# Layer norm of a four-layer graph network: five parts, squares with the mean as bias, subtraction and scaling in one operation

## The reference

```python
def _layernorm(x, axis=-1, eps=1e-05):
    m = jnp.mean(x, axis=axis, keepdims=True)
    v = jnp.var(x, axis=axis, keepdims=True)
    return (x - m) / jnp.sqrt(v + eps)

h = jnp.maximum(_layernorm(x, axis=-1), 0.0)
x = x + _L0_gnn_ref(h, edge_weight, edge_index)          # weighted means over edges, both directions
h = jnp.maximum(_layernorm(x, axis=-1), 0.0)
x = x + _L1_gnn_ref(h, ...)                              # graph convolution, top-2 mixture of 64 experts, batch norm
h = jnp.maximum(_layernorm(x, axis=-1), 0.0)
x = x + _L2_gnn_ref(h, src, dst, L2_gnn_betas)           # four layers of attention by cosine
h = jnp.maximum(_layernorm(x, axis=-1), 0.0)
x = x + _L3_gnn_ref(h, edge_index, ...)                  # three layers of graph attention, four heads
return x
```

## Time and profile before

| what | value |
|---|---|
| median of three runs | 10631.17 us |
| lowest, highest | 10622.68, 10632.24 us |
| the profiled execution's own time | 10520.32 us |
| its span | 10518.6 us |
| mean granted TensorE clock | 0.817 of full speed |
| busy: PE, PEld, DVE, ACT, POOL | 6449.8, 5108.4, 5163.6, 3005.7, 5412.2 us |

### The profile page before, as it was taken

One profiled execution on the slowest core, in us unless ns is written; L12 is line 12 of the kernel. 1 busy time (PEld: TensorE's weight loads), 2 busy tenths in 40 slices (PEclk: granted clock), 3 DMA queues, 4 the chain that ended last, 5 costly groups with the idle time before them and its releaser, 6 DMA issues. The chain is left out here.

```text
span 10518.6 us, 150096 instructions
## 1 busy us (share of the span) xinstructions
PE 6449.8 (61%) x33804; PEld 5108.4 (49%) x33805; DVE 5163.6 (49%) x13884; ACT 3005.7 (29%) x7335; POOL 5412.2 (51%) x5498
## 2 busy tenths in 40 slices
PE   0004434434464872886778688588668868876886
PEld 0003334423342762665666566466546545654554
DVE  7002223341113224555555555555657757775777
ACT  0000000000001221333333333333345545554554
POOL 2766666646641112564555455455436645654563
PEclk9996666666665996998898799899878888888888
DMA  3201113343330981334334333433323333333333
GB/s 135 71 8 41 40 46 85 87 67 93 91 57 22 334 294 49 84 84 74 80 82 81 73 84 82 73 81 82 61 71 82 80 69 78 80 76 67 80 79 66
DMA packets 614773, 886.37 MB, mean 84 GB/s; under 512 B 285685, under 2 KB 423161, under 8 KB 613408
## 3 DMA queue, kind: packets, MB, share of 16 engines
q0 software_dynamic: 241344, 609.84, 26.3%
q1 hardware_dynamic: 373344, 275.70, 8.7%
HBM read 757.50 MB, written 134.33 MB: 85 GB/s over the span
## 5 line engine op out<-in xcount | busy, mean ns | idle before, releaser
L1557 POOL DMA_INDIRECT hs<-tab_agnn,rec x1952 | 1886.2, 966 | 1676.0 <-issue 530.5
L1998 POOL DMA_INDIRECT hs<-tab_gat,rec x1464 | 1516.0, 1036 | 1083.9 <-issue 499.5
L1621 DVE CUSTOM_DVE_ANT_0 prod<-psG,hs 128x256 f32<-128x256 f32 x1952 | 836.3, 481 | 1007.3 <-remote 523.1
L1680 PE MATMUL psG<-HN,ohT 128*128 x3904 | 1097.5, 426 | 109.2 <-DVE lg L1621 74.0
L2030 DVE TENSOR_REDUCE mt<-psL 128x2 f32<-128x1024 f32 x732 | 873.3, 1219 | 477.8 <-remote 208.9
L1697 PE MATMUL psV<-hs,pr 128*128 128x258 f32 x3904 | 1006.6, 404 | 3.3 <-DVE acc L1604 3.3
L1680 PEld LDWEIGHTS psG<-HN,ohT 128*128 128x128 f32 x3904 | 772.8, 210 | 257.4 <-DVE lg L1621 96.6
L2163 PE MATMUL psV<-msg,oh 128*128 128x260 f32 x2928 | 824.5, 431 | 7.2 <-issue 6.8
L1697 PEld LDWEIGHTS psV<-hs,pr 128*128 128x128 f32 x3904 | 759.2, 205 | 104.4 <-DVE acc L1604 4.9
L661 PE MATMUL psT<-ident,oh 128*128 128x128 f32 x488 | 125.1, 406 | 1095.3 <-issue 837.2
L1636 ACT ACTIVATE prT<-cand,mn 128x512 f32<-128x512 f32 x488 | 352.4, 722 | 1519.0 <-DVE mn L1582 1143.3
(11 more groups left out here) (324 smaller groups left out, 12837.2 us busy)
## 6 DMA issues: line engine op xcount, KB each, us to landing
w<-in_L_gnn_w SPq DMA_DIRECT2D x224, 512.0 KB, 5.8
fwd_d<-acc SPq DMA_DIRECT2D x10, 3172.0 KB
fw<-fwd_d SPq DMA_DIRECT2D x122, 260.0 KB
hs<-tab_agnn,rec POOLq DMA_INDIRECT x1952
hs<-tab_gat,rec POOLq DMA_INDIRECT x1464
rec<-rec_d SPq DMA_DIRECT2D x1220, 8.0 KB
b<-in_L_gnn_b SPq DMA_DIRECT2D x113, 128.0 KB, 6.8
x<-xbuf SPq DMA_DIRECT2D x112, 128.0 KB, 6.4
```

The lines of the kernel that those rows point to most:

```text
L1557: nc.gpsimd.indirect_dma_start(out=hs[:, j, g, :], out_offset=None, in_=k.tab_agnn, in_offset=bass.IndirectOffsetOnAxis(ap=rec[:, j, g, 0: ...
L1621: ins = V.tensor_tensor_reduce(prod[:, h2, g, :], psG[:, bank(j2, half), m, :], hs[:, j2, g, 0:D], hs[:, j2, g, D:D + 1], 0.0, ALU.mult, A ...
L1680: mm = nc.tensor.matmul(psG[:, bank(j1, half), m, :], ohT[:, j1 % 2, 2 * half + m, :], pick(HN, b, slice(None)).rearrange("p a c -> p (a c ...
L1998: nc.gpsimd.indirect_dma_start(out=hs[:, j, g, :], out_offset=None, in_=k.tab_gat, in_offset=bass.IndirectOffsetOnAxis(ap=rec[:, j, g, 0:1 ...
```

## The change

A norm works in five parts of five blocks each (`NORM_PARTS`). DVE sums a part, then scales the sums of the part before it to the negative mean, with its own semaphores `ln_sum` and `ln_mean`. ACT waits for each part's mean and squares its five blocks, one activation of 128 x 256 each, straight from `k.X` with the negative mean as a per-partition bias. DVE sums the squares part by part. The variance, the root (now in a tile `root` of its own) and the reciprocal stay whole. DVE then makes (x + negative mean) * rstd for each block in one `tensor_scalar` with two per-partition operands, into `sq`, and signals each part on `ln_out`; ACT's relu follows part by part into `k.H`. The subtraction over all blocks into `k.H` is gone. SP's wait on `ln_h` counts five relus for a norm.

```diff
--- before.py
+++ after.py
@@ -401,7 +401,7 @@
                 for table in tables:
                     sp.dma_start(table[NP:NP + 1, :], zeros[0:1, 0:table.shape[1]]).then_inc(s_zeroed, 16)
                 sp.wait_ge(s_zeroed, (-(-MT // NB) + FILLS + len(tables)) * 16)
-                sp.wait_ge(k.sems.ln_h, norm.n * 2 + 2)
+                sp.wait_ge(k.sems.ln_h, (norm.n + 1) * NORM_PARTS)
                 sp.dma_start(rows(k.tab_bwd[0:NP, :]), k.H[:, :, DH:D]).then_inc(k.sems.ln_st, 16)
                 sp.wait_ge(k.sems.ln_st, 16)
 
@@ -419,6 +419,14 @@
                     pool.wait_ge(s_sent[n], (BATCHES + 1 - n) // 2 * (16 * AHEAD))
 
 
+NORM_PARTS = 5
+
+
+def norm_part(n):
+
+    return slice(n * (NB // NORM_PARTS), (n + 1) * (NB // NORM_PARTS))
+
+
 class Norm:
 
 
@@ -429,32 +437,45 @@
         self.sq = sb("sq", [P, NB, D], F32)
         self.mean = sb("mean", [P, NB], F32)
         self.var = sb("var", [P, NB], F32)
+        self.root = sb("root", [P, NB], F32)
         self.rstd = sb("rstd", [P, NB], F32)
 
     def on_vector(self, dve):
         nc, k, q, n = self.nc, self.k, self.k.sems, self.n
-        sq, mean, var, rstd = self.sq, self.mean, self.var, self.rstd
-        c = Chain(dve, q.ln, n * 6)
-        Hf = k.H[:, :, 0:D]
-        c.done(nc.vector.tensor_reduce(mean[:, :], k.X[:, :, :], AX.X, ALU.add))
-        c.done(nc.vector.tensor_scalar(mean[:, :], mean[:, :], 1.0 / D, None, ALU.mult))
-        c.done(nc.vector.tensor_tensor(Hf, k.X[:, :, :], b3(mean[:, :], D), ALU.subtract))
-        dve.wait_ge(q.ln_sq, n + 1)
-        c.done(nc.vector.tensor_reduce(var[:, :], sq[:, :, :], AX.X, ALU.add))
-        c.done(nc.vector.tensor_scalar(var[:, :], var[:, :], 1.0 / D, LN_EPS, ALU.mult, ALU.add))
+        sq, mean, var, root, rstd = self.sq, self.mean, self.var, self.root, self.rstd
+        V = nc.vector
+        for c in range(NORM_PARTS + 1):
+            if c < NORM_PARTS:
+                V.tensor_reduce(mean[:, norm_part(c)], k.X[:, norm_part(c), :], AX.X, ALU.add).then_inc(q.ln_sum, 1)
+            if c >= 1:
+                dve.wait_ge(q.ln_sum, n * NORM_PARTS + c)
+                V.tensor_scalar(mean[:, norm_part(c - 1)], mean[:, norm_part(c - 1)], -1.0 / D, None, ALU.mult).then_inc(q.ln_mean, 1)
+        for c in range(NORM_PARTS):
+            dve.wait_ge(q.ln_sq, n * NORM_PARTS + c + 1)
+            ins = V.tensor_reduce(var[:, norm_part(c)], sq[:, norm_part(c), :], AX.X, ALU.add)
+        c = Chain(dve, q.ln, n * 3)
+        c.done(ins)
+        c.done(V.tensor_scalar(var[:, :], var[:, :], 1.0 / D, LN_EPS, ALU.mult, ALU.add))
         dve.wait_ge(q.ln_sd, n + 1)
-        c.done(nc.vector.reciprocal(rstd[:, :], mean[:, :]))
-        nc.vector.tensor_tensor(sq[:, :, :], Hf, b3(rstd[:, :], D), ALU.mult).then_inc(q.ln_h, 1)
+        c.done(V.reciprocal(rstd[:, :], root[:, :]))
+        for c in range(NORM_PARTS):
+            for b in range(NB)[norm_part(c)]:
+                ins = V.tensor_scalar(sq[:, b, :], k.X[:, b, :], mean[:, b:b + 1], rstd[:, b:b + 1], ALU.add, ALU.mult)
+            ins.then_inc(q.ln_out, 1)
 
     def on_scalar(self, act):
         nc, k, q, n = self.nc, self.k, self.k.sems, self.n
         sq, mean, var = self.sq, self.mean, self.var
-        act.wait_ge(q.ln, n * 6 + 3)
-        nc.scalar.activation(sq[:, :, :], k.H[:, :, 0:D], ACT.Square).then_inc(q.ln_sq, 1)
-        act.wait_ge(q.ln, n * 6 + 5)
-        nc.scalar.activation(mean[:, :], var[:, :], ACT.Sqrt).then_inc(q.ln_sd, 1)
-        act.wait_ge(q.ln_h, n * 2 + 1)
-        nc.scalar.activation(k.H[:, :, 0:D], sq[:, :, :], ACT.Relu).then_inc(q.ln_h, 1)
+        for c in range(NORM_PARTS):
+            act.wait_ge(q.ln_mean, n * NORM_PARTS + c + 1)
+            for b in range(NB)[norm_part(c)]:
+                ins = nc.scalar.activation(sq[:, b, :], k.X[:, b, :], ACT.Square, bias=mean[:, b:b + 1])
+            ins.then_inc(q.ln_sq, 1)
+        act.wait_ge(q.ln, n * 3 + 2)
+        nc.scalar.activation(self.root[:, :], var[:, :], ACT.Sqrt).then_inc(q.ln_sd, 1)
+        for c in range(NORM_PARTS):
+            act.wait_ge(q.ln_out, n * NORM_PARTS + c + 1)
+            nc.scalar.activation(k.H[:, norm_part(c), 0:D], sq[:, norm_part(c), :], ACT.Relu).then_inc(q.ln_h, 1)
 
 
 def layernorm(nc, k):
@@ -2266,6 +2287,9 @@
         q.e = sem("s_e")
         q.msg3 = sem("s_msg3")
         q.ln = sem("s_ln")
+        q.ln_sum = sem("s_ln_sum")
+        q.ln_mean = sem("s_ln_mean")
+        q.ln_out = sem("s_ln_out")
         q.ln_sq = sem("s_ln_sq")
         q.ln_sd = sem("s_ln_sd")
         q.ln_h = sem("s_ln_h")
```

## The result

The changed kernel takes 10574.93 us in the median of five runs (10571.87 to 10582.52) against 10631.17 for the kernel before (five runs, 10620.65 to 10639.94): 56 us less by the medians. The ratio, estimated from all of these runs and so not simply the quotient of the medians (0.9947), is 0.9951 with a 95% interval of 0.9938 to 0.9964. Forecast were 10584 and a range of 10563 to 10605. The profiled execution lasted 10571.87 us.

The account below looks back on a forecast made before the run. No engine was busy much above half the span: a chain of stages, with three norms exposed between barriers. Three norms' 43.6 us plus 3 for the first, taken as 47, off the median 10631.17 gave 10584 us, range 10563 to 10605.

Parts of the forecast that it names:

- Stretch A: Norm, first sum to last square: subtraction gone, ACT sets the pace; from 19.47 to 13.1 us, 6.4 saved.
- Stretch B: Norm, last square to first scaling, 7.85 us before: only the last second sum stays exposed; 5.3 us saved.
- Stretch C: Norm, scaling and relu: 25 two-pointer instructions, only the last relu behind; from 12.40 to 9.6 us, 2.8 saved.
- The price of its parts: DVE scaling of 256 elements, start to start: 0.136 + 0.067 + 0.06 us for each of two pointers, 0.33 apart.
- The sum: Savings of one norm added up: 14.5 us, from 39.7 to 25.2; three norms between barriers save 43.6.
- The first norm: Norm beside POOL's scatter, its own time hidden: freeing held POOL instructions gains 3 us, between 0 and 11.7.
- Both holds: POOL DMA instructions of 6.43 and 7.16 us, held by DVE's two-input subtraction and product; removing the first frees 5.5 us.
- The total: Whole kernel: 43.6 + 3 = 46.6, taken as 47 us off the median of 10631.17, giving 10584.
- The scaling ran at two elements a cycle: Norm's scaling: rival said one element a cycle, 0.46 us apart, a norm saving 11.2, kernel 10594; chance 0.12.
- The instructions overlapped: Squares and scalings: rival said no overlap, 0.49 and 0.55 us apart, a norm saving 6.8, kernel 10611; chance 0.04.
- The fixed cost of small operations: Objection to small squares and scalings: each SBUF operation pays a fixed cost, tiles of 512 or more advised; counted as included.
- The pace outside the norms: Gather loops: rival said their pace shifts, at the full 111 us giving 10695; chance 0.03, as much for the other sign.

Follow-up runs that it names:

- the probe: Changed kernel plus seven groups of DVE operations and 25 ACT squares behind the first norm, into an unread tile; whole-tile tensor_scalar 3.50 us, 25 small ones 5.91.
- the delayed zeroing: SP's zeroing DMAs held back until 15 scatter batches landed: kernel before 10641.99 us, changed kernel 10582.10 (one run each); changed kernel timed on the other chip, ratio 0.9934.

## Why the prediction was right

**Stretch A** was to end at 13.1 us: the last square ends 2306.36 + 10.08 - 2303.37 = 13.07 behind the start. The pace of ACT, 0.40 a block, was right, and so was the reading that squaring alone becomes dearer.

**Stretch B** was 2.5 and is 2318.89 - 2316.44 = 2.45. **Stretch C** was 9.6 and is 9.47; the scaling's 8.2 is 8.16 (the prediction prints 0.33 apart, which would give 8.34; its unrounded terms, 0.323, give the 8.2). The price of its parts was put together wrongly (0.06 for each pointer; the probe has 0.07 and 0.02, on a base of 0.23 and not 0.20), and the errors cancelled at two pointers: that this term came out so close is luck.

**The sum**, 14.5 a norm and 43.6 for three, is 14.73 and 44.2.

**The first norm** is the term that failed: "I take 3, between 0 and 11.7". It was 0. Both holds went, the second as well, so 11.6 us of POOL's time came free, and all of it went into waits that had stood right behind it in the trace of before. The prediction had allowed for that ("up to the whole") and still taken 3 without a row for it. The Trainium skill's sentence on "SBUF — State Buffer", section "Who interferes with whom", speaks of one instruction, and for one long operation the trace agrees: a DMA instruction of 3.26 us in the probe. The prediction stretched it over 25 short ones, and there it doesn't come out: none of POOL's took over 1.07 beside the new scalings.

**The total**, 47 forecast against 56 measured: 44.2 are shown in the traces. The rest is within what executions of one code differ by. Without the 3 us for the first norm the forecast would have been 10588, well inside the range too, so the error in that term decided nothing.

**The rivals.** The scaling ran at two elements a cycle: 0.32 us apart and not 0.46. The instructions overlapped: squares of 0.49 us started 0.40 apart. The fixed cost of small operations, the Trainium skill's objection on "VectorE: DVE Perf Modes", section on the TRN2 errata, is real (3.50 us in one DVE operation, 5.91 in 25). Together with the price of the pointers it nearly ate the gain of the fusion, as the kernel with one part shows (1.06 us left), but the parts outweigh it. The pace outside the norms proved a larger source of scatter than its 0.03 on either side suggests: 10399.4 to 10563.5 us in two profiles of before. No run shows that the change moves it; the forecast was compared with medians of several executions, which lie much closer together than those two.

## What to carry to other kernels

Where two engines take turns over a whole tile, cutting the tile into parts lets them overlap, and that gives more if the same change takes a pass off the engine that would otherwise be busy throughout: here 8.3 us for the parts, 1.1 for the fusion and 14.7 for both. Before counting time that another engine gains, look at the next wait in its queue: 11.6 us of POOL's vanished into one. And when the stage is 1% of the kernel, measure the stage in the trace, not only the kernel.

## What the runs showed of the hardware that was not expected

A long DVE operation with two inputs (6.82 us), or one at two elements a cycle (3.50 us), holds a POOL indirect DMA instruction begun in it until some 0.85 us behind its own end. With two inputs and 1,280 elements (1.4 us) POOL's instructions take up to 2.07 us, and beside many short fast ones of 0.3 to 0.4 us hardly more than their usual 0.97: 0.97 to 1.07, once 1.11.

The second pointer of a tensor_scalar is nearly free (0.02 us), the first costs 0.07.

In the kernels on the first chip, and in the profiles of the prediction and the result, POOL falls into a slower cadence late in the scatter: its DMA instructions start 1.28 us apart at first and 1.40 from about 555 to 561 us on, with the delayed zeroing only from 706 us (kernel before) and 693 us (changed kernel). Ahead of it the register MOVEs of its queue go from 0.029 us to 0.70: with the early zeroing from about 400 us (all fifteen from 420 to 440 us take 0.70 and start 1.40 apart, while the DMA instructions still start 1.28 apart), with the delayed one from between 500 and 520 us. That the queue has a lead, which it then loses at 0.12 us an instruction, would fit, but no run shows it. On the second chip it never happens: the median and the maximum are 29 ns. This is why the delayed changed kernel ended the stage earlier on the first chip. What sets it off stayed open.

The same code of before took 10652 us on one chip and 9476 on the other, with a granted TensorE clock of 0.811 to 0.819 and of 0.848 to 0.859. The norms of the changed kernel took 24.98 to 25.00 us on both, and its last scatter started at 717 and 704, so nearly all of the difference lies in the stretches of gathers and matmuls; how much of it the clock makes is not shown.
